# A recommendation tower on one core: one-column weights in the last layer, stores per chunk, and another order at the close

## The reference

```python
e = jnp.stack([tbl_0[ids[:, 0]], ..., tbl_25[ids[:, 25]]], axis=1)
z = concatenate([dense, einsum('bfd,bd->bf', e, dense), upper pairs of einsum('bfd,bgd->bfg', e, e)])
h = jnp.concatenate([z, r_dense_features], axis=1)      # 607
h = jnp.maximum(h @ W_top1 + b_top1, 0.0)               # 512
h = jnp.maximum(h @ W_top2 + b_top2, 0.0)               # 256
y = h @ W_top3                                          # 1
```

## Time and profile before

| | |
|---|---|
| median of 3 runs | 373.24 us (372.98 to 373.9) |
| the profiled execution | 373.56 us, span 371.8 us |
| PE busy | 346.7 us, 93% of the span |
| PEld busy | 274.4 us |
| DVE, ACT, POOL busy | 252.6, 176.2, 263.2 us |
| mean granted TensorE clock | 0.982 of full speed |

### The profile page before, as it was taken

How to read it: one execution, slowest core, us unless ns; L and a number is a source line. 1 busy time by engine, 2 the same in 40 slices (tenths; PEclk the granted TensorE clock), 3 DMA queues, 4 the chain that set the end, 5 groups by cost and what they waited for, 6 DMA issues and landing times.

```text
span 371.8 us, 13904 instructions
## 1 busy us (share of the span) xinstructions
PE 346.7 (93%) x5585; PEld 274.4 (74%) x5585; DVE 252.6 (68%) x502; ACT 176.2 (47%) x300; POOL 263.2 (71%) x276
## 2 busy tenths in 40 slices
PE   2899997969999999999999999999899999899987
PEld 0566665757778888887778888887678778779876
DVE  1689889938688773678798753877789672445231
ACT  3366578753613323767514325678213335433332
POOL 6777878777777777777777777777777777777200
PEclk9999999996999999999999999999999999969999
DMA  7999214234333332243333222233333122222100
GB/s 183 247 238 231 66 50 100 54 95 116 94 92 86 86 76 83 60 111 95 91 93 104 86 75 71 75 102 89 97 109 88 51 59 56 56 54 55 26 4 0
DMA packets 21170, 33.51 MB, mean 90 GB/s; under 512 B 8628, under 2 KB 11589, under 8 KB 21107
## 3 DMA queue, kind: packets, MB, share of 16 engines
q0 software_dynamic: 8608, 17.65, 18.7%
q1 hardware_dynamic: 12499, 14.98, 15.4%
HBM read 32.60 MB, written 0.01 MB: 88 GB/s over the span
## 4 chain that ended last, share of the span: by engine, by line
PE 38%; POOL 8%; issue 3%; DMA 2%; ACT 1%; DVE 1%; ACTq 0%
POOL rows L606 8%; PE late_bank L725 7%; PE gram_bank L676 5%; PE turn_bank L657 3%; PE late_bank L630 3%; PE late_bank L631 2%; PE spare_bank L772 2%; PE gram_bank L630 2%; PE gram_bank L631 2%; DMA rows<-in_tbl_dram,index 2%; PE spare_bank L630 1%; PE gram_bank L704 1%; PE turn_bank L630 1%; PE turn_bank L631 1%; PE spare_bank L631 1%
## 5 line engine op out<-in xcount | busy, mean ns | idle before, releaser
L606 POOL DMA_INDIRECT rows<-in_tbl_dram,index x269 | 262.4, 976 | 83.0 <-issue 80.1
L1176 DVE TENSOR_TENSOR one_hot<-table_ids,row_number 125x512 fp32r<-125x512 int32 x216 | 134.5, 681 | 32.7 <-PE gram_bank L631 13.0
L418 ACT COPY turned<-turn_bank 128x512 f32<-128x512 f32 (+1 forms) x69 | 68.1, 1030 | 49.6 <-PE turn_bank L657 45.3
L630 PE MATMUL late_bank<-one_hot,table_hi 125*128 125x512 f32 x168 | 72.9, 434 | 5.4 <-DVE one_hot L1176 3.5
L631 PE MATMUL late_bank<-one_hot,table_lo 125*128 125x512 f32 x168 | 68.5, 408 | 0.0
L676 PEld LDWEIGHTS gram_bank<-turned 128*27 128x27 f32 x4096 | 45.8, 106 | 19.7 <-issue 15.5
L676 PE MATMUL gram_bank<-turned 128*27 128x26 f32 x4096 | 55.4, 193 | 3.4 <-DVE turned L432 1.4
L630 PEld LDWEIGHTS late_bank<-one_hot,table_hi 125*128 125x128 f32 x168 | 32.9, 196 | 20.0 <-issue 5.3
L657 PE MATMUL turn_bank<-ident,rows 128*128 128x128 f32 x285 | 43.5, 277 | 4.4 <-DMA rows<-in_tbl_dram,index 2.8
L657 PEld LDWEIGHTS turn_bank<-ident,rows 128*128 128x128 f32 x285 | 34.9, 142 | 13.7 <-DMA rows<-in_tbl_dram,index 4.3
L1174 DVE TENSOR_SCALAR one_hot<-looked_up,row_number_sb 125x512 fp32r<-125x512 f32 x72 | 32.8, 496 | 12.4 <-issue 6.4
(11 more groups left out here) (138 smaller groups left out, 449.1 us busy)
## 6 DMA issues: line engine op xcount, KB each, us to landing
table_ids<-in_ids_by_table_dram SPq DMA_DIRECT2D x27, 256.0 KB, 3.1
fetched<-in_tbl_dram SPq DMA_DIRECT2D x384, 0.5 KB
rows<-in_tbl_dram,index POOLq DMA_INDIRECT x269
turned<-in_tbl_dram SPq DMA_DIRECT2D x6, 448.0 KB, 13.5
looked_up<-in_tbl_dram SPq DMA_DIRECT2D x3, 448.0 KB, 6.0
rows<-in_r_dense_features_dram SPq DMA_DIRECT2D x16, 64.0 KB, 1.8
gram<-in_W_top_dram SPq DMA_DIRECT2D x1, 702.0 KB
gram<-in_W_top_dram SPq DMA_DIRECT2D x1, 512.0 KB
```

Of the source, the lines that this page charges most:

```text
L418: copy(to[:, f0:f1], of).then_inc(rows_copied[n % 2], 1)
L606: pool.indirect_dma_start(out=rows[:, row % RING_ROWS, :], out_offset=None, in_=tables[f], in_offset=bass.IndirectOffsetOnAxis(ap=index[:, ...
L630: pe.matmul(bank, table_hi[:, s, k, :], hot, start=k == 0, stop=False)
L1176: last = nc.vector.tensor_tensor(hot, table_ids[0:RK, (chunk.n * LOOKUPS + s) % ID_SLOTS, 0:wide], row_number[0:RK, k:k + 1].broadcast_to( ...
```

## The change

The last layer takes one column of `w3_sb` as weights everywhere. For a whole chunk tile t writes to partition 32 t of `y_bank`, 128 columns; for a half, each quarter of the 256 samples (64 columns) writes to its own partition of `last_y_bank`. ScalarE copies 97 partitions. Each whole chunk's output is stored for itself, by a DMA that ScalarE issues; `y`, `turn_outputs`, `copy_output_rows` and `store_rows` are gone. `y_room` is in the room of `gram`, so VectorE waits for the earlier store before it overwrites that place (unit 10). At the close the dense part of FINAL's unit 2 and the early last layer each come one products unit later; FINAL's first unit is written with all high parts as soon as they are there, and the low parts one k later; layer2(0) comes after three units; and VectorE makes the second half of the last hidden layer.

```diff
+FINAL_LAYER2_AFTER = ((), (), (0,), (1, 2))
...
+            if chunk.n > 0 and chunk is not LAST and n == Y_UNIT:
+                engine.wait_ge(stored, chunk.n * DMA)
...
-            def store_rows():
-                sp.wait_ge(y_rows_copied, 1)
-                sp.dma_start(out[0:LAST.first * P, :].rearrange("(n p) o -> n (p o)", p=P), y_rows).then_inc(stored, DMA)
...
             def store_half(part):
                 sp.wait_ge(y_copied, part.n + 2)
-                sp.dma_start(out[part.first * P:(part.first + part.tiles) * P, :].rearrange("b n -> n b"),
-                             last_y[:, samples_of(part)]).then_inc(stored, DMA)
+                sp.dma_start(out[part.first * P:(part.first + part.tiles) * P, :].rearrange("(g b) n -> g (b n)", g=GROUP),
+                             y_quarters[0:P:QUAD, y_of(part)]).then_inc(stored, DMA)
...
-                    if g == 0:
-                        pe.wait_ge(y_rows_copied, 1)
...
+            def final_first_layer1():
+                for k in range(1, K1):
+                    pe.wait_ge(pairs_hi_made, FINAL.n * K_PAIRS + k)
+                    for w in (w1_hi, w1_lo):
+                        pe.matmul(h1_bank(FINAL, 0), w[0:height(k), k, 0:P], input_hi[0:height(k), k, samples_of(FINAL)],
+                                  start=False, stop=False)
+                    if k > 1:
+                        pe.wait_ge(pairs_split, FINAL.n * K_PAIRS + k - 1)
+                        pe.matmul(h1_bank(FINAL, 0), w1_hi[0:PK, k - 1, 0:P], input_lo[0:PK, k - 1, samples_of(FINAL)],
+                                  start=False, stop=False)
+                pe.wait_ge(pairs_split, (FINAL.n + 1) * K_PAIRS)
+                pe.matmul(h1_bank(FINAL, 0), w1_hi[0:PK, K1 - 1, 0:P], input_lo[0:PK, K1 - 1, samples_of(FINAL)],
+                          start=False, stop=True).then_inc(h1_summed, 1)
...
             def layer3(part):
                 pe.wait_ge(h2_made, (part.n + 2) * N2)
-                for t in range(part.tiles):
-                    for k in range(N2):
-                        last = pe.matmul(y_bank[:, t:t + 1], h2_of(part, k)[:, t * P:(t + 1) * P], w3_sb[:, k:k + 1],
+                for k in range(N2):
+                    for t in range(part.tiles):
+                        last = pe.matmul(y_bank[t * QUAD:t * QUAD + 1], w3_sb[:, k:k + 1], h2_of(part, k)[:, t * P:(t + 1) * P],
                                          start=k == 0, stop=k == N2 - 1)
...
                 for k in range(N2):
-                    pe.wait_ge(h2_made, (part.n + 1) * N2 + k + 1)
-                    last = pe.matmul(last_y_bank[:, 0:width(part)], w3_sb[:, k:k + 1], h2_of(part, k), start=k == 0, stop=k == N2 - 1)
+                    if part is FINAL and k == 1:
+                        pe.wait_ge(last_h2_made, 1)
+                    else:
+                        pe.wait_ge(h2_made, (part.n + 1) * N2 + k + 1)
+                    for g in range(GROUP):
+                        samples = slice(g * HALF * QUAD, (g + 1) * HALF * QUAD)
+                        last = pe.matmul(last_y_bank[g * QUAD:g * QUAD + 1], w3_sb[:, k:k + 1], h2_of(part, k)[:, samples],
+                                         start=k == 0, stop=k == N2 - 1)
                 last.then_inc(y_summed, 1)
-            def turn_outputs():
-                pe.wait_ge(y_copied, LAST.n + 1)
-                pe.transpose(y_rows_bank, y[:], ident[:]).then_inc(y_turned, 1)
...
                 products(LAST, 3, 0)
+                products(LAST, 3, 1)
                 dense_ahead(FINAL, 2)
-                products(LAST, 3, 1)
+                products(LAST, 3, 2)
                 half_layer3(EARLY)
-                products(LAST, 3, 2)
                 products(LAST, 3, 3)
...
-                for n in range(N1):
+                final_first_layer1()
+                for n in range(1, N1):
                     layer1(FINAL, n)
-                    for k in LAYER2_AFTER[n]:
+                    for k in FINAL_LAYER2_AFTER[n]:
                         layer2(FINAL, k)
...
+            def store(chunk):
+                act.wait_ge(y_copied, chunk.n + 2)
+                act.dma_start(out[chunk.first * P:(chunk.first + TILES) * P, :].rearrange("(t b) n -> t (b n)", t=TILES),
+                              (closing_y_room if chunk is CLOSING else y_room)[0:P:QUAD]).then_inc(stored, DMA)
...
-                for n in range(N2):
-                    relu2(FINAL, n)
+                relu2(FINAL, 0)
                 copy_output(FINAL)
...
+                dve.wait_ge(h2_summed, (FINAL.n + 1) * N2)
+                nc.vector.tensor_scalar(h2_of(FINAL, 1), h2_bank(FINAL, 1), b2_sb[:, 1:2], 0.0, ALU.add, ALU.max).then_inc(last_h2_made, 1)
```

More of the change, by code:

```diff
@@ L1008, in copy_output @@
                 if part.tiles < TILES:
[L1009 to L1011 removed]
+                    high = (GROUP - 1) * QUAD + 1
+                    nc.scalar.copy(y_quarters[0:high, y_of(part)], last_y_bank[0:high]).then_inc(y_copied, 1)
+                else:
+                    high = (TILES - 1) * QUAD + 1
+                    nc.scalar.copy((closing_y_room if part is CLOSING else y_room)[0:high], y_bank[0:high]).then_inc(y_copied, 1)
+            def store(chunk):
+                act.wait_ge(y_copied, chunk.n + 2)
+                act.dma_start(out[chunk.first * P:(chunk.first + TILES) * P, :].rearrange("(t b) n -> t (b n)", t=TILES),
+                              (closing_y_room if chunk is CLOSING else y_room)[0:P:QUAD]).then_inc(stored, DMA)
             def work_off(chunk, following):
@@ L1025, in work_off @@
                             copy_output(CHUNKS[chunk.n - 1])
+                            store(CHUNKS[chunk.n - 1])
                         if u == 1 and t < TILES - 2:
```

30 lines of the change are left out of this document (12 added, 18 removed).

## The result

Before 373.96 us (median of 20 runs, 372.87 to 375.61), after 375.24 us (20 runs, 372.65 to 377.7): ratio 1.0031 [1.0016, 1.0046]. The kernel became 1.2 us slower by the ratio (1.28 in the medians), where I had forecast 0.85 us faster, and lies above my range. Part of the distance to the forecast of 372.4 us is the base: it started from three runs with a median of 373.24, and over 20 runs the kernel before has 373.96. The profiled execution took 374.57 us, 372.4 of it in the span; for before it was 373.56 and 371.8. So 0.6 us came into the span, and 0.4 us outside it (2.17 us against 1.76). The changed kernel's times also spread more: 5.05 us between its fastest and its slowest run, where the kernel before has 2.74, and its fastest run is as fast as the other's.

What follows compares the result with a forecast made beforehand. Gathers were taken to pace TensorE until 347.55, then only a chain of TensorE work. Terms -0.03 + 0.20 - 0.34 - 0.12 - 0.56 = -0.85 us gave a median of 372.4 us, range 371.4 to 374.0.

Steps and rivals of the forecast that it cites:

- the closing computation: From the end of TensorE's pause in the closing products to the copy's end: steps forecast at -0.82 us together.
- The bound now: Gathers pace TensorE until row group 3 at 347.55; the 24.2 us after it are held by nothing else.
- Last layer of the whole chunks: One-column weights in whole chunks save 0.2 to 1.5 us a chunk, all of it going into the wait before 324.79.
- turn_outputs: Dropping a transpose, copy and store between 327.4 and 347.55 saves 0.03 us, at most 0.35, at least nothing.
- Order of the closing products: Early last layer comes behind a pause whose end is fixed: +0.20 us for everything behind, +0.80 if groups don't overlap.
- rival B: The pause in the closing products keeps its 0.88 us wherever the layer stands: sum -1.7, 371.55 us; chance 0.20.
- Rival C: One-column weights don't overlap between column groups, early layer +0.80: sum +0.04, 373.3 us; chance 0.08.
- Rival D: TensorE's clock falls to 1.2 GHz at about 355.8, adding about 2.8 us: sum +2.0, 375.2 us; chance 0.12.
- First unit: Final part's first unit, high parts first, lets the next unit start sooner: 0.34 us saved at most, at least 0.
- layer2(0): In the final part, one more unit before layer2(0) hides its hand-over: -0.12 us, between 0 and -0.15.
- The end: Final stretch: second ReLU -0.07, last layer -0.34, copy -0.15, store in four pieces taken 0 (0 to +0.1); together -0.56 us.
- Around the span: Time of the profiled execution outside the span, 1.76 us in the kernel before, given no term in the sum.

Runs made afterwards that it cites:

- e9: Changed kernel with the whole chunks' last layer computed three times over (48 passes instead of 16): 375.26 us, ratio 1.0031 to the kernel before.
- c2: Changed kernel with two steps of single-row fetches (16 of 96 rows) moved ahead of the load of dense tile 15: 373.93 us, ratio 1.0011.
- c1: Changed kernel without edit, on the same chip as c2: 374.98 us, ratio 1.0036 to the kernel before.
- e1: Changed kernel with the whole chunks' stores issued by SP instead of ScalarE: 376.57 us, ratio 1.0063 to the kernel before.
- e4: Changed kernel run again without edit: 376.37 us, ratio 1.0048 to the kernel before.
- e8: Kernel before with only the whole chunks' part: one-column last layer, stores per chunk from ScalarE, no turn_outputs: 374.6 us, ratio 1.0009.
- s2: Changed kernel with two single-row fetch steps moved ahead of the load of dense tile 15, an earlier run than c2: 373.73 us, ratio 0.999.
- a2: Kernel before with only VectorE's second ReLU of the change: 372.91 us in its single run.
- b1: Kernel before with two fetch steps moved earlier and the change's first unit and layer2(0), but ScalarE's ReLU: 373.65 us, ratio 0.9993.
- e3: Changed kernel with the dense part and the early last layer back in the old closing order: 376.17 us, ratio 1.0054 to the kernel before.
- e2: Changed kernel with the whole chunks as before (layer3, turn_outputs and joint store back): 375.3 us, ratio 1.0032 to the kernel before.
- s4: Kernel before with its two closing stores reading four partitions instead of one, copy unchanged: 374.89 us, ratio 1.0011.
- a3: Kernel before with its joint store of twelve rows cut into three of four rows, all from SP: 374.32 us in its single run.

## Why the prediction was wrong

**The steps that failed.** The terms that I worked out, the closing computation, gave -0.58 us for -0.82. What made the kernel slower were terms that I put at nothing: the store in four pieces (0, measured 0.46), the time around the span (carried over unchanged, measured +0.41), and in the stretch ahead of the pause the sentence that saved work only makes a wait longer and is "worth nothing", with the one that nothing else holds TensorE from 347.55 on. The new layer of the whole chunks costs some 0.6 to 0.7 us there, through the stream of single rows. Of the 2.8 us between the forecast 372.4 and the measured 375.24, 0.7 are the base, as said above.

**The bound now.** "The gathers hold TensorE" was right, and e9 shows it. "From 347.55 to the end ... nothing else holds; only that stretch can give time back" missed the second stream: row group 4 of the last tile waits for SP's single rows too. In the profile of before the last of their issues ends at 347.64, 1.42 us ahead of group 4 at 349.06; where group 4 did wait, it is 1.00 to 1.21. So the pin was there with a cushion of 0.2 to 0.4 us. I looked at GpSimd's stream and not at SP's. Timelines of before, the last fetches of the stream and the weight loads of group 4:

```profile
337.17 10.47 SPq L535 DMA_DIRECT2D fetched<-in_tbl_dram  x21
...
349.06 0.14 PEld L657 LDWEIGHTS turn_bank<-ident,rows 128*128 128x128 f32 x1
...
349.17 0.14 PEld L657 LDWEIGHTS turn_bank<-ident,fetched 128*128 128x128 f32 x1
```

I also left out group 4's own gather, the last one at 345.83; by the landing times that I used it would be there between 348.42 and 349.43. It proved to be no bound (2.76 us in c2).

**Last layer of the whole chunks.** The size was right: about 0.66 us for sixteen passes, between the bounds. "Worth nothing" was right as a gain (e9 puts the work back and loses nothing) and failed as a cost. Saved time went into the waits as I said, but I priced the chunks' whole part at zero. The counts of long runs show that this part costs and that the stream carries the cost; that lateness at tile 12 reaches group 4 by the stream is shown by c1 and c2 and by the 1.0 us that separate the two whenever group 4 waits. What makes TensorE late at tile 12 is not shown. A spell at 1.2 GHz behind the longer wait goes with it in five profiles of nine (c1, c2, e1, e4, e8), but e9 was late without one. Which piece of the chunks' part does it (the passes, the copy of 97 partitions, the stores and the wait for them) was not separated, except that the queue of the stores is not the cause (e1).

**turn_outputs.** -0.03 forecast: from the wait at 328.03 to row group 3 at 348.36 TensorE took 20.33 us, before 20.16; nothing gained. The wait of 0.3 us for a gather which I named as a sign was not in this profile; a longer one (0.8 to 1.4 us) is in c1, c2, e4, e8, e9 and s2, and with the old chunk layer in a2 and b1.

**Order of the closing products.** Right in size, +0.22 for +0.20. Only 0.08 of it is the order: with the old order but the layer in four groups (e3) that step takes 1.61 us, 0.14 more than before, because the layer's sixteen passes now stand ahead of the pause and push more products behind it (106 weight loads for 95). Right in what fixes the end of the pause, as far as can be told: in all twenty profiles it comes 4.6 to 5.4 us after group 4 is turned, whichever order stands behind it (mean 4.9 with the old order, 5.0 with the new), and the pause lasts 0.23 to 1.13 us with the old order and 1.14 to 1.62 with the new. So it does not keep its length, and rival B is out. That it waits for a block of instructions is still my reading; no run tests it. Rival C is out with 16 passes in 0.22 us, and so is the estimate of 16 x 25 ns = 0.40 us. (By my own terms that estimate would have made the sum about -0.6 us, with 0.15 more in the early layer and 0.09 in the last. I had written -0.5.) Rival D happened in two of the eight profiles with the new order (e4, e9) and in none of the twelve with the old; it cost 1.1 us in e4 and 1.4 in e9, where I had worked out 2.8.

**First unit.** -0.23 for -0.34. The last low part was made at 362.34, its matmul came 0.11 us later and the next unit 0.16 after that: 0.27 where I had counted 0.18.

**layer2(0).** -0.09 for -0.12.

**The end.** The last layer and the copy exactly as worked. VectorE's ReLU gained nothing: it takes 0.48 us and not the 0.42 of a subtraction of the same width. The store was mis-sized: I gave it 0 with an upper bound of 0.1, and it costs 0.46. The row at hand (0.23 us of issue for one piece) bounded nothing for four pieces. The issue alone goes up by 0.27 us with three more pieces. The Trainium skill (DMA: Bandwidth & Descriptors, "Anatomy of one DMA — SWDGE (gpsimd) path") says of DMAs that GpSimd issues that many descriptors can be emitted before their cost shows. Carried over to this store, which SP issues, that would have meant no added cost, and the trace shows one.

**Around the span.** I carried 1.76 us over as a constant. It became 2.17, and this is a third of the loss. The experiments place it (0.35 with the chunks' part alone, 0.2 with the first unit and VectorE's ReLU together) and do not explain it. It can't be seen in a trace, which is a reason to give it a term with a range.

Together: -0.58 closing chain, +0.46 store, +0.4 around, +0.6 to 0.7 by the stream, which is 0.9 to 1.0 of the measured 1.2 us. The sum is not a closed account: e2, without the stream's part, should by this sum have lost nothing, and by its ratio it lost 1.2 us, at least 0.3.

## What to carry to other kernels

Before saying that a stretch is held by nothing, list every stream that feeds it, single-row DMAs on the quiet queue too, and look when the last of its issues ends against the use, not only whether a wait shows. A part that can save nothing can still cost: here the chunks' part made one run in three over 2 us late, because a stream is paced by TensorE's position far ahead of the end. Look at the spread of all runs, not only at the median and one profile; and before two single profiles are compared, find how far their gathers stand apart to begin with. Cutting a final result over several partitions must be weighed with its store: 0.49 us were saved in the layer and the copy, and 0.46 went into the pieces.

## What the runs showed of the hardware

A store of 1 KB from four partitions instead of one takes SP 0.50 us instead of 0.23 to issue, and the span ends 1.98 us after the copy instead of 1.52 (after and s4 against before). Single-column weights with 64 moving columns in four column groups: sixteen passes in 0.22 us (after, 355.26 to 355.48). Single rows fetched by SP, 0.52 us apart in the mean, could be used 1.00 to 1.21 us after the end of the last issue (eight profiles). GpSimd's gathers keep nearly the same distances in all profiles but start up to 2.4 us apart from one execution to the next (324.43 to 326.78). The time outside the span keeps within 0.08 us of its median for most kernels (1.80, 2.15, 2.20) and moves by 0.2 to 0.4 us between kernels that differ in a few instructions, which neither the queue used (e1) nor the number of stores (a3) explains. A TensorE that waits 3 us for data at 262 fell to 1.2 GHz afterwards in c1, c2, e1 and e4 and kept 2.4 in e3, in executions of nearly the same program.
